# Two attentions and a mixture of experts on one core: a hand-placed order of steps replaced by a greedy one

## The chip, the core and the metric

One NeuronCore of a Trainium2 chip runs the whole program. It has five in-order instruction queues: TensorE (PE, with weight loads shown apart as PEld), VectorE (DVE), ScalarE (ACT), GpSimd (POOL) and SyncE (SP), which here only issues transfers. The metric is device time in microseconds (us), the median of several runs.

## The reference

The input x is 2 batches of 1024 tokens by 128 channels, in float32. The layer is, with all weights small:

```
x = layernorm(x + attention0(x))                  # 8 heads of 16, causal, plus a rank-one geometric bias
x = layernorm(x + ffn(x)), where ffn(x) is y with
    h = rmsnorm(x, norm1_w)
    q = rope(h Wq);  latent = layernorm(h Wdkv) * ln_g + ln_b   (64 wide)
    k = rope(latent Wuk);  v = latent Wuv
    x = x + softmax(causal(q k / sqrt(8))) v Wo   # 16 heads of 8
    g = rmsnorm(x, norm2_w)
    e = argmax(g gate_w + gate_b)                 # one of 4 experts per token
    y = x + W2[e] relu(W1[e] g + b1[e]) + b2[e]   # 512 hidden; all 4 experts are computed, one is picked
```

## The kernel before

Work is cut into **steps**, tuples such as `("scores", F, v)` or `("proj", M, 0)`. One global list, SCHEDULE, holds all of them. Each engine's program walks this list in order and emits the instructions of the steps in which it has a part, with semaphore waits for what it reads. The list thus sets the order on every queue; it does not set any time.

**Attention groups.** A group F is 4 heads of one batch: groups 0 and 1 are attention 0 of batch 0, groups 2 and 3 of batch 1, groups 4 to 7 attention 1 of batch 0, groups 8 to 11 of batch 1. For a group there are 38 `max` units (a matmul of queries against keys without the row maximum, L837, with a causal mask matmul L834, then a maximum on VectorE, L1238); then `combine`, `turnmax` (transpose L894 and a split into three bf16 parts) and `rows` (three DMAs put the negated maxima as rows into qs). Only then can the 38 `scores` units run (matmul L858, exponential on ScalarE L1024 into pr), `mask` on GpSimd (L752) for diagonal blocks, `pv` (12 products per group, L875), and per half of the queries `evac` (ScalarE, L1029) and `turn` (transposes L886, then reciprocal and product on VectorE, into att). Keys and queries of a group sit in one of three slots (qs, ks), filled by `load` DMAs from DRAM scratch.

**Chains.** Before attention 0, `before_first(b)` transposes x (`feed`, L912; `feat`), projects it (`proj`, L931), splits q and k into three bf16 parts (`hi`, `r1`, `mid`, `lo`) and stores them. Between the attentions, `between(b)` goes from the last `turn` of attention 0 of a batch to the stored q and k of attention 1. It handles both halves (512 tokens each) of the batch together: transposes of att, output product `y`, `residual`, `moments`, inverse root (`root`, four parts of linked small VectorE instructions, L1169 to L1176), `layer_norm` into x1 (L1281), `square` on ScalarE (L1070), `square_sum` on VectorE (L1288), a second root, `hat` on GpSimd (L792), transposes, `latent` and its normalisation (a third root), four rotated blocks M of q and k (`proj`, `rotate` L1313 on VectorE, `rotated` L773 on GpSimd through one buffer), their split and store, and the values. `ready` and `experts` do the same after attention 1, with `hidden` (L1004), `relu` (L1089) and `expert` (L948).

**The order around the change.** `backbone` writes the attention steps in a fixed pattern. A product follows the scores of its step by LAG = 2 steps. The maxima of group G are spread evenly over the run of group G-1, by MAX_SPREAD. The chains are spread evenly between two positions, where position F is the start of group F's scores: before_first(1) from -0.5 to 0.4, between(0) from 2.21 to 3.12, between(1) from 4.21 to 5.95, ready(0) and its experts from 8.21 to 11.7, ready(1) half 0 from 11.71, experts of batch 1 from 13. At 12.9 stands `quiet`, from where all eight PSUM banks serve the experts.

## Time and profile before

| | before |
|---|---|
| median of 3 runs | 675.29 us (673.31 to 678.19) |
| profiled execution | 673.76 us |
| its span in the trace | 671.9 us |
| mean granted TensorE clock | 0.954 |
| TensorE busy | 582.0 us (87%) |
| VectorE busy | 413.1 us (61%) |
| ScalarE busy | 337.8 us (50%) |
| GpSimd busy | 145.5 us (22%) |

The span runs from the first to the last instruction in the trace. Busy is time in which an engine has an instruction in work; a clock of 1 is 2.4 GHz, 0.5 is 1.2 GHz, and a value between is a mean over the stretch.

### The profile page before, as it was taken

The numbers are of one execution on the slowest core, as the hardware profiler recorded it, in microseconds if no ns is written. First come the engines' busy times: TensorE is split into PE (matmuls) and PEld (weight loads), VectorE is DVE, ScalarE is ACT, GpSimd is POOL, SyncE is SP. The second block draws the span as 40 slices with busy tenths as digits, with TensorE's granted clock in tenths as the row PEclk, the third lists the DMA queues.
The fourth block names the chain that finished last, engine by engine and source line by source line (L and its number), as shares of the span: only waits on it lengthen the run. The fifth ranks groups of instructions, "written<-read, shape, count | busy, mean of one in ns | idle before, by whom it ended". The sixth has DMA issues, their size and how long they took to land.

```text
span 671.9 us, 10096 instructions
## 1 busy us (share of the span) xinstructions
PE 582.0 (87%) x3668; PEld 279.0 (42%) x3717; DVE 413.1 (61%) x1031; ACT 337.8 (50%) x621; POOL 145.5 (22%) x186
## 2 busy tenths in 40 slices
PE   5578899958777877879999999999989999799994
PEld 3224233424223233424433344455544545357663
DVE  3496987796615968897778878754566402422313
ACT  4234457544463454557766667545546555633330
POOL 7612112313371031135321214011012011101000
PEclk9798899978787998999999999999999999989997
DMA  4856020000044020031313030220000000000000
GB/s 141 210 159 219 26 73 25 2 1 0 32 116 75 1 65 0 3 64 48 85 28 60 6 65 0 31 35 1 2 0 18 2 0 1 17 0 1 17 1 16
DMA packets 27394, 27.69 MB, mean 41 GB/s; under 512 B 6289, under 2 KB 22545, under 8 KB 27090
## 3 DMA queue, kind: packets, MB, share of 16 engines
q1 hardware_dynamic: 26962, 26.26, 16.2%
q0 software_dynamic: 384, 0.79, 0.5%
q8 instruction: 30, 0.49, 0.3%
q14 instruction: 18, 0.15, 0.1%
HBM read 19.40 MB, written 7.34 MB: 40 GB/s over the span
## 4 chain that ended last, share of the span: by engine, by line
PE 64%; DVE 20%; DMA 4%; issue 4%; ACT 4%; POOL 2%; SPq 1%; DVEq 0%; ACTq 0%; POOLq 0%
PE ps L875 13%; PE ps L948 10%; PE ps L858 10%; DVE mparts L1238 10%; PE ps L837 9%; PE ps L1004 8%; PE ps L834 3%; PE ps L937 3%; PE ps L931 2%; ACT pr L1024 2%; DMA qs<-nparts 2%; PE ps L912 2%; PE ps L946 2%; PE ps L886 1%; DVE stats L1147 1%
## 5 line engine op out<-in xcount | busy, mean ns | idle before, releaser
L1024 ACT ACTIVATE pr<-ps 128x512 f32<-128x512 f32 (+1 forms) x456 | 250.3, 576 | 227.9 <-PE ps L858 192.1
L1238 DVE TENSOR_REDUCE mparts<-ps 128x1 f32<-128x512 f32 (+3 forms) x456 | 279.9, 655 | 112.4 <-PE ps L837 111.2
L837 PE MATMUL ps<-ks,qs 125*128 125x512 bf16 (+3 forms) x576 | 170.0, 337 | 12.6 <-DVE mparts L1238 11.1
L858 PE MATMUL ps<-qs,ks 128*128 128x512 bf16 (+3 forms) x532 | 154.6, 332 | 15.7 <-ACT pr L1024 9.2
L752 POOL TENSOR_SCALAR_AFFINE_SELECT pr<-pr 128x512 f32<-128x512 f32 x96 | 61.0, 636 | 369.1 <-ACT pr L1024 368.9
L875 PE MATMUL ps<-pr,vs 128*32 128x512 f32 (+3 forms) x1152 | 126.4, 512 | 0.4 <-POOL pr L752 0.4
L858 PEld LDWEIGHTS ps<-qs,ks 128*128 128x128 bf16 x576 | 50.8, 99 | 143.2 <-ACT pr L1024 92.5
L834 PE MATMUL ps<-cmask,identb 128*128 128x128 bf16 (+2 forms) x259 | 64.9, 251 | 26.9 <-DVE mparts L1238 12.5
L837 PEld LDWEIGHTS ps<-ks,qs 125*128 125x128 bf16 x576 | 55.4, 100 | 53.1 <-DVE mparts L1238 21.2
L948 PE MATMUL ps<-w,work 128*128 128x128 f32 x512 | 74.1, 288 | 0.0
L1089 ACT ACTIVATE work<-ps,b 128x512 f32<-128x512 f32 x64 | 43.8, 686 | 49.1 <-PE ps L1004 48.5
L1004 PE MATMUL ps<-feat,w 128*128 128x512 f32 x128 | 63.9, 608 | 2.6 <-DVE att L1142 1.7
L948 PEld LDWEIGHTS ps<-w,work 128*128 128x128 f32 x512 | 61.9, 191 | 4.3
L834 PEld LDWEIGHTS ps<-cmask,identb 128*128 128x128 bf16 x264 | 26.3, 100 | 54.3 <-DVE mparts L1238 35.1
L1327 DVE SCALAR_TENSOR_TENSOR xn<-ps,onehot,xn 128x128 f32<-128x128 f32 x48 | 13.5, 344 | 48.0 <-PE ps L948 48.0
L875 PEld LDWEIGHTS ps<-pr,vs 128*32 128x32 f32 x1152 | 23.0, 109 | 46.9 <-issue 23.5
L1004 PEld LDWEIGHTS ps<-feat,w 128*128 128x128 f32 x128 | 23.6, 196 | 15.9 <-issue 12.6
L1138 DVE RECIPROCAL rc<-ps 128x16 f32<-128x16 f32 x24 | 6.1, 255 | 34.2 <-PE ps L886 33.8
L886 PE MATMUL ps<-ident,ot 128*128 128x128 f32 x96 | 16.9, 304 | 2.8 <-DVE mparts L1238 1.8
L946 PE MATMUL ps<-b2p,ones 3*128 3x128 bf16 x64 | 14.3, 224 | 3.7 <-ACT work L1089 3.6
L792 POOL TENSOR_TENSOR xn<-x,rstd 128x512 f32<-128x512 f32 x8 | 8.2, 1039 | 43.1 <-DVE rstd L1176 43.1
L785 POOL TENSOR_TENSOR parts<-work,parts 128x512 bf16<-128x512 f32 x12 | 13.9, 1156 | 13.9 <-ACT parts L1053 13.8
(119 smaller groups left out, 391.5 us busy)
## 6 DMA issues: line engine op xcount, KB each, us to landing
qs<-scr1q SPq DMA_DIRECT2D x64, 64.0 KB
ks<-scr1k SPq DMA_DIRECT2D x64, 64.0 KB
qs<-scr0q SPq DMA_DIRECT2D x48, 64.0 KB, 2.3
ks<-scr0k SPq DMA_DIRECT2D x36, 64.0 KB, 2.2
scr0q<-parts SPq DMA_DIRECT2D x4, 384.0 KB, 2.8
scr0k<-parts SPq DMA_DIRECT2D x4, 384.0 KB, 3.2
scr1q<-parts SPq DMA_DIRECT2D x4, 384.0 KB, 2.5
scr1k<-parts SPq DMA_DIRECT2D x4, 384.0 KB, 2.6
```

The costliest lines, as they stand in the source:

```text
L752: pool.affine_select(out=p, in_=p, compare_op=ALU.is_ge, fill=0.0, base=0, pattern=[[0, HG], [1, P]], channel_multiplier=-1).then_inc(done ...
L834: pe.matmul(bank[:, :, w - P:w], identb[:, :], cmask[:, 0:nh, :], start=True, stop=False, skip_group_check=True)
L837: last = pe.matmul(bank[:, h, :], queries(F, KMAX, h0 + h, i * P, P), ks[0:KMAX, F % SLOTS, h0 + h, 512 * c:512 * c + w], start=not diagon ...
L858: last = pe.matmul(to[:, h, :], ks[0:KEXP, F % SLOTS, h0 + h, j * P:(j + 1) * P], queries(F, KEXP, h0 + h, qb * 512 + lo, n), start=True, ...
L875: last = pe.matmul(ps[VW * h:VW * (h + 1), PVB, lo:lo + n], vs[:, F % VSLOTS, j, VW * h:VW * (h + 1)], pr[:, st % PSLOTS, h, 0:n], start=( ...
L886: last = pe.transpose(bank[:, t * P:(t + 1) * P], ot[:, q, t * P:(t + 1) * P], ident[:, :])
L946: pe.matmul(to, ones3[0:3, :], b2p[0:3, e * C:(e + 1) * C], start=True, stop=False, skip_group_check=True)
L948: last = pe.matmul(to, hid[:, e % 2, c, t * P:(t + 1) * P], w2[:, e * HC + c, :], start=False, stop=(c == HC - 1), skip_group_check=True)
L1004: pe.matmul(side(*step), w1[:, c * P:(c + 1) * P], feat[:, columns(b, i)], start=True, stop=True).then_inc(done["hidden"], 1)
L1024: act.activation(pr[:, st % PSLOTS, h0:h0 + nh, 0:STEPS[st][3]], scores_at(F, v), ACT.Exp, scale=GROUPS[F][0].scale).then_inc(exped, 1)
L1089: act.activation(hid[:, c // HC % 2, c % HC, :], side("hidden", b, i, c), ACT.Relu, bias=b1[:, c:c + 1]).then_inc(done["relu"], 1)
L1238: dve.tensor_reduce(mparts[:, F % SLOTS, h0:h0 + nh, i, c], maxes_at(F, u), AX_X, ALU.max).then_inc(taken, 1)
```

## The change

The positions stay as wishes only. `wanted` gives each step a position and each stream of dependent steps a lane, whose order is kept. `order` then builds SCHEDULE: it keeps a model of when each engine is free and when each step ends, from the table COSTS and the dependencies in `needs`, and repeatedly takes, among the heads of all lanes, the step with the smallest (wait in us on its first engine + 1.0 x its position). The maxima of a group may be wanted 1.2 groups ahead.

The chain between the attentions is cut in halves of 512 tokens, `between(b, i)`, each with its own roots. The first rms norm is folded into the layer norm: for x1 the root is taken of two values at once, 1/sqrt(v + eps) and 1/sqrt(v (1 + 1e-6) + 1e-11), and `hat0` on VectorE writes the doubly normalised values directly from xn; `square`, `square_sum`, the root and `hat` of the first rms norm go. x1 itself is written by four GpSimd instructions at the end of the chain. Blocks M of attention 1 are numbered half by half, and group 4 too is loaded in halves (HALVED). `ready(b, i)` works by halves as well. Products no longer have a fixed lag. The table's durations for scores, max and pv are linear in the columns; `halves_of_array` always gives both.

The diff, cut to its core (`needs`, which lists for each step kind the steps it reads from, the lanes and the changed semaphore waits are left out):

```diff
+def between(b, i):
+    q = block_of(1, b, 0, i)
+    k = block_of(1, b, 1, i)
+    return [("feed", "att0", b, i), ("feat", "att0", b, i), ("y", 0, b, i), ("residual", 0, b, i), ("moments", 0, b, i),
+            *root("x1", b, (i,)), ("hat0", b, i), ("feed", "hat0", b, i), ("feat", "hat0", b, i),
+            ("latent", b, i), ("lat_copy", b, i), ("proj", q, 0), ("rotate", q, 0), ("lat_moments", b, i),
+            *root("latent", b, (i,)), ("lat_norm", b, i), ("proj", q, 1), ("rotate", q, 1), ("rotated", q),
+            ("lat_turn", b, i), ("lat_feat", b, i), ("hi", q), ("r1", q), ("mid", q), ("lo", q), ("store", q),
+            ("proj", k, 0), ("rotate", k, 0), ("proj", k, 1), ("rotate", k, 1), ("rotated", k),
+            ("hi", k), ("r1", k), ("mid", k), ("lo", k), ("store", k), ("v_proj", 1, b, i), ("v_out", 1, b, i), ("x1", b, i)]
...
+MAX_AHEAD, MAX_LENGTH = 1.2, 0.9
-SECOND = (-0.5, 0.4)
-BETWEEN = [(2.21, 3.12), (4.21, 5.95)]
-AFTER = (8.21, 11.7)
-LAST = (11.71, 12.4)
+FIRST = [[(-2.0, -1.5), (-1.6, -1.1)], [(-0.5, 0.0), (-0.1, 0.4)]]
+BETWEEN = [[(1.2, 1.21), (2.0, 2.01)], [(3.4, 4.9), (4.1, 5.6)]]
+READY = [[(7.4, 7.9), (8.1, 8.4)], [(11.4, 11.6), (12.1, 12.2)]]
+EXPERTS = [[(7.9, 9.7), (9.7, 11.4)], [(11.6, 13.0), (13.0, 14.0)]]
...
+PE, DVE, ACTE, POOL, SP = "pe", "dve", "act", "pool", "sp"
+HOP = 0.07
+AFTER_ISSUE = {PE: 0.17, DVE: 0.0, ACTE: 0.0, POOL: 0.0, SP: 2.2}
+URGENT = 1.0
+def halves_of_array(step):
+    return 0, 1
+COSTS = {"feed": (PE, 0.58), "feat": (ACTE, 0.6), "proj": (PE, 0.87), "rotate": (DVE, 0.7), "rotated": (POOL, 1.27),
+         "hi": (ACTE, 0.62), "mid": (ACTE, 0.63), "store": (SP, 0.42), "v_proj": (PE, 1.14), "v_out": (ACTE, 0.6),
+         "combine": (DVE, 0.3), "rows": (SP, 1.0), "mask": (POOL, 0.64), "evac": (ACTE, 0.6), "y": (PE, 1.14),
...
+START = {PE: 5.0, DVE: 6.5, ACTE: 1.0, POOL: 6.4, SP: 4.5}
+X_READY = [5.0, 6.0, 7.0, 8.0]
...
+def order(wanted):
+    lanes = {}
+    for pos, stream, step in sorted(wanted, key=lambda e: e[0]):
+        lanes.setdefault(lane(stream, step), []).append((pos, step))
+    for name in lanes:
+        if name[0] == "projections":
+            lanes[name].sort(key=lambda e: e[1][1])
+    out, end, emitted_max = [], {}, {}
+    free = dict(START)
+    tile_free, issued, last_tile = [START[PE]] * 2, START[PE], None
+    ring, exps = [], []
+    bank_free, bank_reader, bank_use = {}, {}, {}
+    bank_held = {}
+    def ready(step, shared):
+        if kinds_left(step):
+            return None
+        times = []
+        for need in needs(step):
+            if need not in end:
+                return None
+            times.append(end[need] + HOP)
+        kind = step[0]
+        first = costs(step)[0][0]
+        if kind == "feed" and step[1] == "x":
+            times.append(X_READY[2 * step[2] + step[3]])
+        if kind in ("max", "turn", "turnmax"):
+            if len(ring) >= MAXN:
+                times.append(ring[-MAXN] + HOP)
+        if kind == "scores":
+            st, h0, _ = UNITS[step[2]]
+            if len(exps) >= SCN:
+                times.append(exps[-SCN] + HOP)
+            elif (SCB + step[2]) in bank_reader and bank_reader[SCB + step[2]] not in end:
+                return None
+            serial = step[1] * NS + st - PSLOTS
+            if serial >= 0 and ("pv", serial // NS, serial % NS) not in end:
+                return None
+        if kind == "pv" and step == ("pv", 0, 0) and PVB in bank_reader and bank_reader[PVB] not in end:
+            return None
+        if kind == "expert" and step[4]:
+            pass
+        elif kind in READER or kind == "proj":
+            bank = choose(shared)
+            if bank is None:
+                return None
+            if bank in bank_reader:
+                times.append(end[bank_reader[bank]] + HOP)
+        if first == PE:
+            own = halves_of_array(step) if kind in ("scores", "max") else (0, 1)
+            times += [tile_free[t] for t in own] + [issued]
+        else:
+            times.append(free[first])
+        at = max(times)
+        return at - max(issued, 0 if first == PE else free[first]), at
+    def kinds_left(step):
+        if step[0] == "combine":
+            F, q = step[1:]
+            return emitted_max.get(F, 0) < (NX0 if q == 0 else NX)
+        return False
+    def choose(shared):
+        able = [b for b in shared if b not in bank_reader or bank_reader[b] in end]
+        return min(able, key=lambda b: bank_use.get(b, -1)) if able else None
+    shared = [0, 1, *SIDE, PVB]
+    while any(lanes.values()):
+        best = []
+        for name, waiting in lanes.items():
+            if not waiting:
+                continue
+            picks = [0]
+            if name[0] == "max" and last_tile is not None:
+                F = name[1]
+                left = min(len(waiting), 6)
+                same_half = [k for k in range(left) if (waiting[k][1][2] < NX0) == (waiting[0][1][2] < NX0)]
+                picks = [k for k in same_half if last_tile not in halves_of_array(waiting[k][1])][:1] or [0]
+            for k in picks:
+                at = ready(waiting[k][1], shared)
+                if at is not None:
+                    best.append((at[0], waiting[k][0], name, k, at[1]))
+        _, pos, name, k, at = min(best, key=lambda x: max(x[0], 0.0) + URGENT * x[1])
+        step = lanes[name].pop(k)[1]
+        out.append(step)
+        kind, time = step[0], at
+        if kind == "scores" and step[1] == 0 and step[2] == 0:
+            shared = SIDE
+        if kind == "quiet":
+            shared = list(range(8))
+        if kind in READER or kind == "proj":
+            if not (kind == "expert" and step[4]):
+                bank = choose(shared)
+                bank_use[bank] = len(out)
+                if kind == "proj":
+                    bank_reader[bank] = ("r1", step[1]) if step[1] < 8 else ("rotate", step[1], step[2])
+                else:
+                    bank_reader[bank] = (READER[kind],) + step[1:4]
+        for k, (engine, cost) in enumerate(costs(step)):
+            if k:
+                time = max(time + HOP, free[engine])
+                if kind == "scores":
+                    serial = step[1] * NS + UNITS[step[2]][0] - PSLOTS
+                    if serial >= 0:
+                        time = max(time, end["pv", serial // NS, serial % NS] + HOP)
+            if engine == PE:
+                own = halves_of_array(step) if kind in ("scores", "max") else (0, 1)
+                issued = time + cost if len(own) == 2 else time
+                for t in own:
+                    tile_free[t] = time + cost
+                last_tile = own[0] if len(own) == 1 else None
+                if kind not in ("scores", "max"):
+                    last_tile = None
+            else:
+                free[engine] = time + cost
+            time += cost + AFTER_ISSUE[engine]
+        end[step] = time
+        if kind == "weights":
+            end[step] += 6.0
+        if kind in ("max", "turn", "turnmax"):
+            ring.append(time)
+        if kind == "max":
+            emitted_max[step[1]] = emitted_max.get(step[1], 0) + 1
+        if kind == "scores":
+            exps.append(time)
+    return out, end
+SCHEDULE, ENDS = order(wanted())
+MAX_ORDER = [[s[2] for s in SCHEDULE if s[:2] == ("max", F)] for F in range(NF)]
...
+                elif kind == "x1":
+                    b, i = args
+                    pool.wait_ge(done["root"], nth("root", "x1", b, (i,), 3))
+                    for t in range(TB * b + 4 * i, TB * b + 4 * i + 4):
+                        last = pool.tensor_scalar(x1[:, t, :], xn[:, t, :], mv[:, t, 0:1], rstd[:, 2, t:t + 1],
+                                                  ALU.subtract, ALU.mult)
+                    last.then_inc(done["x1"], 1)
...
-                    if of[:3] == "rms":
-                        dve.wait_ge(done["square_sum"], nth("square_sum", int(of[3]), b, blocks[-1]))
+                    if of == "rms1":
+                        dve.wait_ge(done["square_sum"], nth("square_sum", b, blocks[-1]))
+                        link(dve.tensor_scalar(rstd[:, 1, t], rstd[:, 5, t], 1.0 / C, RMS_EPS, ALU.mult, ALU.add))
                     elif of == "latent":
-                        dve.wait_ge(done["lat_moments"], nth("lat_moments", b, 1))
+                        dve.wait_ge(done["lat_moments"], nth("lat_moments", b, blocks[-1]))
+                        link(dve.tensor_scalar(rstd[:, 1, t], lat_mv[:, t, 1], 1.0, LN_EPS, ALU.mult, ALU.add))
                     else:
-                        which = 0 if of == "x1" else 2
-                        dve.wait_ge(done["moments"], nth("moments", which, b, blocks[-1]))
-                    link(dve.tensor_scalar(v, src, scale, eps, ALU.mult, ALU.add))
+                        dve.wait_ge(done["moments"], nth("moments", 0 if of == "x1" else 2, b, blocks[-1]))
+                        if of == "x1":
+                            link(dve.tensor_scalar(rstd[:, 1, t], mv[:, t, 1], 1.0 + RMS_EPS, LN_EPS * RMS_EPS, ALU.mult, ALU.add))
+                        link(dve.tensor_scalar(rstd[:, 0, t], mv[:, t, 1], 1.0, LN_EPS, ALU.mult, ALU.add))
...
+                elif kind == "hat0":
+                    b, i = args
+                    dve.wait_ge(done["root"], nth("root", "x1", b, (i,), 3))
+                    for t in range(TB * b + 4 * i, TB * b + 4 * i + 4):
+                        last = dve.tensor_scalar(x0[:, t, :], xn[:, t, :], mv[:, t, 0:1],
+                                                 rstd[:, 3, t:t + 1], ALU.subtract, ALU.mult)
+                    last.then_inc(done["hat0"], 1)
```

## Rows read from the trace of the kernel before

**Rows 1.** The page: span, and busy time, share and instructions of each engine.

```profile
span 671.9 us, 10096 instructions
...
PE 582.0 (87%) x3668; PEld 279.0 (42%) x3717; DVE 413.1 (61%) x1031; ACT 337.8 (50%) x621; POOL 145.5 (22%) x186
```

**Rows 2.** Windows: stretch, length, busy us of PE, PEld, DVE, ACT, POOL; clock, DMA share, GB/s.

```profile
0.00:38.50 38.50, 20.09 (x84) 10.82 (x86) 19.62 (x39) 11.91 (x21) 25.56 (x38) 0.91 0.64 171
38.50:98.10 59.60, 50.75 (x307) 19.45 (x310) 50.28 (x98) 27.83 (x53) 8.58 (x12) 0.94 0.37 117
98.10:129.50 31.40, 30.62 (x221) 11.65 (x224) 25.45 (x49) 21.11 (x41) 7.81 (x10) 1.00 0.10 27
129.50:196.00 66.50, 48.60 (x275) 22.79 (x280) 40.33 (x130) 31.89 (x61) 24.37 (x25) 0.83 0.11 28
196.00:209.00 13.00, 9.49 (x61) 4.02 (x62) 2.04 (x5) 5.81 (x12) 5.21 (x6) 0.76 0.52 98
209.00:246.50 37.50, 31.31 (x192) 11.18 (x193) 31.20 (x58) 16.10 (x30) 4.66 (x5) 0.97 0.20 38
246.50:334.60 88.10, 78.12 (x527) 34.74 (x535) 72.48 (x191) 52.75 (x101) 28.50 (x33) 0.98 0.17 40
334.60:397.20 62.60, 61.24 (x440) 23.20 (x447) 50.06 (x95) 42.02 (x81) 10.90 (x18) 1.00 0.21 37
397.20:549.30 152.10, 146.21 (x953) 75.32 (x968) 86.21 (x209) 84.01 (x156) 20.88 (x31) 1.00 0.08 13
549.30:585.90 36.60, 31.78 (x232) 16.15 (x233) 10.95 (x50) 20.97 (x39) 6.74 (x9) 1.00 0.03 8
585.90:672.00 86.10, 73.81 (x386) 49.67 (x385) 24.53 (x114) 23.34 (x35) 2.31 (x2) 0.92 0.02 7
```

**Rows 3.** The chain that ended last, 129.5 to 250: start us, us, what.

```profile
146.56 1.19 DVE rstd L1288 x2
...
151.64 1.05 POOL xn L792
...
188.65 1.27 POOL work L773
...
199.76 5.80 DMA ks<-scr1k
...
219.35 7.48 DVE mparts L1238 x13
```

**Rows 4.** The timeline of ScalarE, the two evacuation copies of group 1.

```profile
106.72 0.58 ACT L1029 COPY ot<-ps 128x512 f32<-128x512 f32 x1
...
128.84 0.58 ACT L1029 COPY ot<-ps 128x512 f32<-128x512 f32 x1
```

**Rows 5.** Groups by line: busy us, mean ns, idle before. Last two from 246.5:334.6 alone.

```profile
L1238 DVE TENSOR_REDUCE mparts<-ps 128x1 f32<-128x512 f32 (+3 forms) x456 | 279.9, 655 | 112.4 <-PE ps L837 111.2
...
L792 POOL TENSOR_TENSOR xn<-x,rstd 128x512 f32<-128x512 f32 x8 | 8.2, 1039 | 43.1 <-DVE rstd L1176 43.1
...
L1281 DVE TENSOR_SCALAR x<-xn,mv,rstd 128x128 f32<-128x128 f32 x16 | 4.9, 368 | 0.0
...
L1281 DVE TENSOR_SCALAR xn<-xn,mv,rstd 128x128 f32<-128x128 f32 x16 | 4.5, 342 | 0.1
...
L931 PE MATMUL ps<-work,wuk 128*128 128x512 f32 x8 | 4.2, 601 | 0.0
...
L992 PE MATMUL ps<-ident,work 128*64 128x128 f32 x8 | 1.2, 273 | 0.0
```

**Rows 6.** The timeline at the end: last matmuls, first instruction after moments, normalisation, store.

```profile
662.03 1.16 PE L948 MATMUL ps<-w,work 128*128 128x128 f32 x8
...
665.71 0.17 DVE L1169 TENSOR_SCALAR rstd<-mv 128x4 f32<-128x4 f32 x1
...
668.09 1.11 DVE L1281 TENSOR_SCALAR xn<-xn,mv,rstd 128x128 f32<-128x128 f32 x4
669.23 0.37 SPq L688 DMA_DIRECT2D out<-xn  x1
```

More of the change, by code:

```diff
@@ new lines, in attention @@
+    for F in range(NF):
+        passed, done = 0, {}
+        for v, (st, _, nh) in enumerate(UNITS):
+            out.append((F + passed / total, ("scores", F, v)))
+            passed += nh * STEPS[st][3]
+            done[st] = F + passed / total
+        for st in range(NS):
+            if STEPS[st][4]:
+                out.append((done[st], ("mask", F, st)))
+            out.append((done[st], ("pv", F, st)))
+            if st in END:
+                q = END.index(st)
+                out += [(done[st], ("evac", F, q)), (done[st], ("turn", F, q))]
@@ L338 @@
           "gate": "pick", "hidden": "relu", "expert": "pick_up"}
-LONG = {"layer_norm": 1.5, "hat": 2.0, "lat_norm": 2.0, "moments": 1.5, "pick": 1.5}
 def spread(steps, first, last):
-    total, passed, out = sum(LONG.get(s[0], 1.0) for s in steps), 0, []
-    for s in steps:
-        out.append((first + (last - first) * passed / total, s))
-        passed += LONG.get(s[0], 1.0)
-    return out
-def loads(position, F):
-    if F >= ATT[0].groups:
-        return [(position, ("load", F, k, 2)) for k in range(2)]
-    return [(position, ("load", F, k, i)) for i in range(2) for k in range(2)]
@@ L383, with halves_of_load, wanted, add @@
-SECOND = (-0.5, 0.4)
-BETWEEN = [(2.21, 3.12), (4.21, 5.95)]
-AFTER = (8.21, 11.7)
-LAST = (11.71, 12.4)
-SCHEDULE = schedule()
+    return [(first + (last - first) * k / len(steps), s) for k, s in enumerate(steps)]
+def halves_of_load(F):
+    return (0, 1) if F in HALVED else (2,)
+def wanted():
+    out = [(pos, "attention", s) for pos, s in attention() + maxima_steps()]
+    def add(stream, steps):
+        out.extend((pos, stream, s) for pos, s in steps)
+    for b in range(B):
+        for i in range(2):
+            add(("first", b, i), spread(before_first(b, i), *FIRST[b][i]))
+            add(("before", b, i), spread(between(b, i), *BETWEEN[b][i]))
+            add(("after", b, i), spread(ready(b, i), *READY[b][i]))
+            add("result", spread(experts(b, i), *EXPERTS[b][i]))
+    for F in range(NF):
+        for half in halves_of_load(F):
+            add("loads", [(max(-1.05, F - 1.9) + 0.01 * half, ("load", F, k, half)) for k in range(2)])
+    add("loads", [(F - 0.5, ("copy_v", F)) for F in range(NF)])
+    add("once", [(0.05, ("weights",)), (0.6, ("b2_parts",)), (0.7, ("partners",)),
+                 (-1.99, ("pads", 0)), (-1.98, ("pads", 1)), (-0.62, ("pads", 2)), (NF + 0.9, ("quiet",))])
+    add("once", [(F - 2, ("zeros", F)) for F in range(ATT[0].groups, ATT[0].groups + SLOTS)])
+    return out
@@ new lines, with lane @@
+OWN_LANE |= {kind: kind for kind in ("hidden", "relu", "expert", "pick_up", "x1", "x12", "scores", "pv", "mask", "copy_v", "quiet",
+                                     "pads", "zeros", "weights", "b2_parts", "partners")}
+def lane(stream, step):
+    kind = step[0]
+    if kind in ("max", "load"):
+        return step[:4] if kind == "load" else step[:2]
+    if kind in ("hi", "r1", "mid", "lo", "store"):
+        return "split", step[1]
+    if kind in ("proj", "rotate", "rotated", "v_proj", "v_out"):
+        return OWN_LANE[kind], step[1] >= (8 if OWN_LANE[kind] == "projections" else 1)
+    return OWN_LANE.get(kind, stream)
```

439 lines of the change are left out of this document (241 added, 198 removed).

## Prediction

> **What bounds the kernel now.** I read the clock and busy totals first, then a table of windows cut at the ends of attention groups, then the chain of work inside the worst window, then single durations. The totals [rows 1] name TensorE: 582.0 of 671.9 us busy, and no other engine over 61%. So an order of steps can win at most what TensorE idles (89.9 us), and what its clock loses when it idles. The profiled execution took 673.76 us, 1.86 us more than its span; the median of the runs is 675.29 us, 1.5 us above it. I make the sum against the span.
>
> The windows [rows 2] show where the idle time lies. A quiet stretch is 334.6 to 397.2: two groups (6 and 7) that do scores, products and maxima for a later group, with no other stream, in 62.6 us, TensorE busy 61.24. So a **plain group** is worth 31.3 us and has no slack left. Elsewhere:
> - 129.5 to 246.5 (three rows: 66.5, 13.0 and 37.5 us, together 117.0 us) is groups 2 and 3, with the chain between the attentions for batch 0 inside. TensorE is busy 48.60 + 9.49 + 31.31 = 89.4 us, so 27.6 us idle, and the granted clock falls to 0.83, 0.76 and 0.97: a mean of c between its two levels 1 and 0.5 costs (1 - c) of the window, here 11.3 + 3.1 + 1.1 = 15.5 us in which full-speed work was not done (part of it idle time as well).
> - 246.5 to 334.6 (88.1 us) is groups 4 and 5, with the same chain for batch 1: the same steps, 10.0 us idle, clock 0.98.
> - 0 to 98.1: 27.3 us idle, clock 0.91 and 0.94, with VectorE busy 50.28 of 59.6 us in its second part.
> - 397.2 to 585.9: 5.9 + 4.8 us idle. The tail from 585.9: 12.3 us idle, of which the last 9.9 us can't go: the last matmuls start at 662.03 and everything behind is one serial run of VectorE and a store [rows 6].
>
> In the worst window the chain of waits [rows 3] reads as one dependency after another: two square sums on VectorE, the GpSimd product by the root, half blocks rotated through one buffer, the copies of ks that land 5.80 us after 199.76, and only then 13 maxima back to back on VectorE. While those loads are awaited, 196 to 209, VectorE is busy 2.04 of 13.0 us. The maxima of group 4 cannot start before 205.6, and group 4 cannot score before they are done. The bound here is the latency of the chain for batch 0, from the last turn of group 1 at 129.5 to 205.6: 76 us.
>
> **The change, part by part.** 1. *The chain for batch 0 starts earlier and by halves.* The old order holds both halves until position 2.21. The first half needs only the first turn of group 1, whose evacuation copy is at 106.72; the second copy is at 128.84 [rows 4]. The new order asks for half 0 from 1.2 and half 1 from 2.0, so half 0 gets a lead of 22 us. Half 1 keeps its start but loses steps: the square sums from 146.56 to the end of the GpSimd product at 152.69 are 6.1 us, and a square before them; I take 8 us. One k block, not two, is rotated behind the second latent transpose (two such additions on GpSimd start some 5 us apart, one of them at 188.65 [rows 3]): 5 us. The steps that run for both halves in turn become single; some thirteen lie on the path (transposes, copies, projections, residual, moments, normalisations), each near the 0.6 us of a square sum (1.19 for two [rows 3]): 8 us, an estimate. 76 - 21 = 55 us, so the second halves of ks for group 4 land near 185. Behind that are the 27 maxima of the later query tiles at 0.655 us [rows 5] = 17.7 us, and about 7 us for combine, transpose, split and the row DMAs (219.35 + 7.48 to the start of group 4 at 246.5 has these and ten more maxima). Group 4 could start near 210, where it now starts at 246.5: 36 us.
>
> 2. *Is there engine time for it?* TensorE: two plain groups are 62.6 us and the chain's matmuls are 18.3 us (eight groups of rows in the window of batch 1; the largest and the smallest are in [rows 5]), 81 us against 117.0: 36 us again. VectorE: the window has 40.33 + 2.04 + 31.20 = 73.6 us busy, plus what is added, minus what moves into group 1 (25.45 of 31.4 busy, so 6 us of room): it would then be 90% busy. An end from below: groups 4 and 5 take 88.1 us with the same content. That is 29 us less than 117.0. I take 28 us, close to the stretch that really ran, because group 1 will be lengthened by what moves into it. Ends: 12 and 37.
>
> 3. *The chain for batch 1* moves from 4.21-5.95 to 3.4-4.9 and 4.1-5.6. Its window is 88.1 us against 81 us of matmuls: 4 us, ends -3 and 7.
>
> 4. *Start-up and groups 0 and 1.* The same chain of projection, split, store and load leads to the first scores; finer interleaving changes little, and VectorE is 84% busy from 38.5 to 98.1 with maxima that all must be done. 2 us, ends -4 and 6.
>
> 5. *Groups 8 to 11 and the tail.* The first experts of batch 1 may run from 11.6, in the last group (4.8 us idle of 36.6), where they now wait for 13. 4 us from the groups and 2 us from the tail, ends 0 and 9.
>
> 6. *Steps added and removed.* There are 16 inverse roots in place of 13: four each for x1, latent, second rms and result, where x1, first rms, latent and second rms had 2, 2, 2 and 3. One takes 668.09 - 665.71 = 2.38 us on VectorE [rows 6], so 7.1 us more, and one more small instruction in each of the four x1 roots (0.2 us each). Four square sums of 0.6 us go, and four squares on ScalarE. Net about +5.5 us on VectorE, in windows where it is 60 to 82% busy: 1 us on the path. The product of the first rms leaves GpSimd (1.04 us each [rows 5]), and the normalised x1 comes onto it, four instructions per half; their price isn't in the trace, between 0.2 us each (a fifth of the full product) and 1.04 us each. I take 0.4, 1.6 us a half, off the chain. A mask queued behind one waits that long, and a product with it: at most 4 x 4 us, taken as 0 because ScalarE runs ahead. The loads of group 4 become four in place of two, so 16 more DMA issues on SP in a queue idle there: 0.
>
> In the trace, the normalisation that runs with GpSimd active (x, at 368 ns) is 26 ns longer per instruction than the same one in the final result (342 ns) [rows 5]. The Trainium skill ("SBUF — State Buffer", Who interferes with whom) says that VectorE and GpSimd share one port pair under an exclusive lock, so that the second blocks fully. That speaks against moving x1 to GpSimd beside VectorE's hat0; By that rule the sixteen instructions of hat0 and those of x1 would run one after the other, up to 16 x 0.368 = 5.9 us. By the rows it is 16 x 0.026 = 0.4 us. The sum takes neither.
>
> 7. *The price of a greedy order.* Every queue is in order; where a real duration is longer than the table's, what is planned behind it waits. The table's maxima (0.1 + 512/880 = 0.68) and hidden steps agree with the trace; a matmul at the half clock takes twice what it says. I charge 3 us, ends 0 and 60 (below).
>
> Sum: 28 + 4 + 2 + 6 - 1 - 3 = 36 us. 671.9 - 36 = 635.9 of span, 637.8 us of time; I give **638**.
>
> **The rivals.** *VectorE or the chain takes the place of the wait.* The maxima of groups 2, 3 and 4 and two half chains meet on one in-order VectorE, and the latent roots of half 0 delay the maxima of group 2. For it: 13 maxima back to back on the chain [rows 3] and 81% in group 1. Against: batch 1's stretch keeps TensorE 89% busy at 82% of VectorE. It gives 12 us of the 28, and 4 us from the last groups: 671.9 - 12 - 4 + 3 + 1.9 = 661 us. *The whole forecast gain and the full bounds.* 37 + 7 + 4 + 8 and no misfit: 671.9 - 56 + 1.9 = 618 us.
>
> *Slower: the greedy rule undoes the lead of scores over products.* The old order keeps each product two steps behind its scores, whatever the durations, and plain groups are 98% busy [rows 2]. The greedy one places a product as soon as the table says the exponential and mask are done. There are 456 score units and 144 products; if each waits 0.1 us more because the real release is later than planned, that is 60 us, and the gain of 39 before misfit turns into 671.9 + 60 - 39 + 1.9 = 695 us. It decides from a mean wait of 0.065 us. Against it: a hand-over in the trace is short (the last normalisation ends at 669.20, its store is issued at 669.23 [rows 6], where the table allows 0.07), and maxima are nearly always at hand to fill a wait. *The order in effect stays as it was*, because the same dependencies release the same steps: 669 to 675.
>
> **Chances.** Forecast (626 to 650) 0.50; VectorE in its place (650 to 667) 0.22; the full gain 0.10; no effect 0.07; slower 0.11. The likeliest is 638. The range leaves out the slower case and no effect (0.18 together) and little more: 617 to 664. A difference of 1% is what can be told from none here; faster by more 0.82, within it 0.07, slower 0.11.
>
> **What would show it.** Group 4's first scores near 215 in place of 246.5; no window in 129.5 to 215 with VectorE under 30% busy; mean clock above the present 0.954; plain groups 6 and 7 still 31 to 32 us each; 16 roots; TensorE busy still near 580 minus what the clock gives back, at over 90% of the span. The prediction is wrong if the plain groups grow by more than 2 us each with TensorE waiting on exponentials, if the second half of ks lands after 200, or if the maxima of group 4 finish late because VectorE has no gap.

## The result, and the profile after

The changed kernel takes 656.07 us (median of 4 runs, 651.37 to 657.64) against 676.15 us for the kernel before (4 runs, 673.31 to 678.19). The ratio is 0.969, 95% interval 0.963 to 0.976. That is 20.1 us or 3.1% faster. The forecast was 638 us, 37 us under the 675.29 us it started from, so about half of it came.

The page of the changed kernel, which answers to [rows 1]:

```profile
span 649.6 us, 10160 instructions
...
PE 572.1 (88%) x3664; PEld 278.2 (43%) x3717; DVE 423.2 (65%) x1067; ACT 335.9 (52%) x617; POOL 153.8 (24%) x198
```

TensorE is 9.9 us less busy for nearly the same instructions, at a mean granted clock of 0.967 where the kernel before had 0.954; its idle time fell from 89.9 to 77.5 us. This page is of the fastest of the four executions. The other three had clocks of 0.950 to 0.953, and a second profiled execution of the same kernel (c0 below, clock 0.955) shows TensorE busy 577.2 us and idle 78.5. So the fall in idle time stands in both, and about half of the 9.9 us belongs to this one execution. VectorE is 10.0 us busier and GpSimd 8.3 us.

A second evacuation copy (ScalarE, line 1276 here, 1029 before) closes each group. The two of group 1, answering to [rows 4], and the second of group 0 stand in the timeline of ScalarE of the changed kernel:

```profile
105.35 0.58 ACT L1276 COPY ot<-ps 128x512 f32<-128x512 f32 x1
114.79 0.58 ACT L1276 COPY ot<-ps 128x512 f32<-128x512 f32 x1
152.01 0.58 ACT L1276 COPY ot<-ps 128x512 f32<-128x512 f32 x1 [0.37 <-PE ps L1119]
```

Subtracting the starts of successive second copies gives a length for every group. The rows of the changed kernel and of c0 are two executions of the same kernel. Groups 2, 3, 4, 6, 7 and the rest repeat to within 0.2 us, so there the table places an effect more sharply than the total does. Groups 0, 1 and 5 differ by 2.6, 2.1 and 1.2 us between the two, so a difference of that size there says nothing (us; groups 8 to 11 taken together; spans of one profiled execution each):

| kernel | group 0 | 1 | 2 | 3 | 4 | 5 | 6 | 7 | 8 to end of span |
|---|---|---|---|---|---|---|---|---|---|
| before | 97.5 | 31.3 | 66.6 | 50.4 | 48.7 | 39.4 | 31.3 | 31.3 | 275.4 |
| changed | 105.4 | 46.7 | 49.6 | 37.4 | 43.2 | 37.8 | 31.1 | 36.3 | 262.3 |
| c0, changed again | 107.9 | 48.8 | 49.5 | 37.4 | 43.4 | 39.0 | 31.1 | 36.3 | 262.3 |
| e1, rows first | 96.0 | 46.9 | 49.6 | 37.4 | 43.2 | 37.8 | 31.1 | 36.3 | 262.3 |
| e3, half 0 held | 106.2 | 31.9 | 56.8 | 39.7 | 43.4 | 39.7 | 31.1 | 36.3 | 262.3 |
| e6, both | 95.9 | 31.9 | 56.8 | 39.7 | 43.4 | 38.6 | 31.1 | 36.3 | 262.3 |
| e8, table corrected | 97.7 | 47.4 | 49.4 | 36.0 | 41.5 | 39.7 | 30.3 | 36.3 | 262.3 |
| e5, halves by hand | 97.5 | 31.3 | 72.2 | 51.1 | 63.0 | 37.8 | 31.3 | 31.3 | 279.3 |
| e7, weight 10 | 95.5 | 32.6 | 89.2 | 37.4 | 45.7 | 36.6 | 32.9 | 37.3 | 275.2 |

From before to changed: group 0 +7.8, groups 1 to 3 together -14.7, groups 4 and 5 -7.1, groups 6 and 7 +4.7, the rest -13.1, in sum -22.3 us, the difference of the two spans. Groups 2 and 3 alone lost 30.0 us, but 15.4 of these are back in group 1. The last two terms belong together too: experts now start in group 7, which lengthens it, and from the start of group 6 to the end 8.4 us are gained.

The windows of the changed kernel, cut close to its own group ends, answer to [rows 2] (columns as there):

```profile
0.00:43.70 43.70, 25.95 (x111) 13.99 (x113) 22.46 (x44) 14.07 (x24) 27.30 (x40) 0.88 0.74 160
43.70:106.00 62.30, 43.20 (x273) 15.49 (x276) 45.37 (x90) 23.41 (x44) 6.15 (x9) 0.86 0.30 97
106.00:152.70 46.70, 40.27 (x258) 17.05 (x262) 37.28 (x100) 25.41 (x48) 17.80 (x20) 0.96 0.15 43
152.70:202.30 49.60, 43.31 (x266) 19.53 (x269) 39.58 (x104) 25.79 (x48) 19.99 (x21) 0.93 0.14 43
202.30:239.60 37.30, 35.35 (x249) 15.53 (x251) 32.23 (x81) 23.60 (x46) 9.60 (x11) 1.00 0.19 33
239.60:320.70 81.10, 74.02 (x504) 32.10 (x512) 71.26 (x174) 50.03 (x96) 31.52 (x39) 1.00 0.17 47
...
537.20:580.50 43.30, 39.25 (x250) 18.86 (x253) 13.60 (x59) 26.16 (x48) 7.38 (x10) 1.00 0.02 7
580.50:649.60 69.10, 59.35 (x329) 40.84 (x328) 21.90 (x101) 18.86 (x28) 2.30 (x2) 0.96 0.03 8
```

The three windows from 106.0 to 239.6 idle TensorE for 14.7 us at a clock of 0.93 and more; the matching stretch before idled it 28.4 us at down to 0.76. TensorE's work there is nearly the same, 118.9 us against 120.0. Of the 14.7 us, 5.3 end with work of ScalarE (4.5 of it exponentials), 4.5 with VectorE and 3.1 with a mask on GpSimd, each in waits of 2.1 us or less: no engine stands out. VectorE is busy 82% of these windows, 67% before. The second row is the surprise: 19.1 us idle and clock 0.86 in group 0, where the kernel before had 8.9 us at 0.94. The chain of waits, read inside that window, shows one hole:

```profile
56.88 9.14 DMA scr0q<-parts
66.03 0.34 SPq L858
...
68.76 2.62 DMA scr0k<-parts
71.40 0.30 SPq L858
...
74.09 0.55 SPq L908
...
75.32 1.76 DMA qs<-nparts
77.08 0.45 issue
77.53 0.63 PE ps L1102
```

A store of projected q is issued on SyncE at 56.88 and takes 9.14 us to land. Behind it on the same in-order queue stands a load of group 2 that reads it, then the next store, then a load that reads that one, and only at 74.09 the row DMAs (L908) with the negated maxima of group 0. These had been ready since 59.5 (the last split instruction on VectorE starts at 59.24 and takes 0.28), and group 0's second half of scores waits for them.

The slow landing isn't new. In the kernel before, the same kind of store, issued behind the same bulk loads, took 9.1 us too (last number of its line in the list of transfers issued from 43 to 60 us):

```profile
scr0q<-parts SPq DMA_DIRECT2D x1, 384.0 KB, 9.1
```

The timeline of SyncE there:

```profile
47.59 0.49 SPq L660 DMA_DIRECT2D scr0q<-parts  x1
54.65 1.82 SPq L671 DMA_DIRECT2D qs<-nparts  x3
...
57.13 3.48 SPq L621 DMA_DIRECT2D qs<-scr0q  x6
```

The rows (L671) left while that store was still on its way, and the loads that read it stood behind them. What is new is the order on the queue. The window of the hole in the changed kernel:

```profile
60.40:77.50 17.10, 1.21 (x4) 0.33 (x4) 5.60 (x13) 0.00 (x0) 0.00 (x0) 0.59 0.52 171
```

TensorE does 1.21 us of work in 17.1, ScalarE and GpSimd none, and the mean granted clock is 0.59.

### The profile page after: what moved, and what is told of

Same layout as the page of the kernel before. It is cut to its first block, busy times and chain, and to the rows that moved or that the text cites. A ratio compares the mean times of both kernels' runs of the same rounds, so it can differ in the third digit from the quotient of the medians.

```text
span 649.6 us, 10160 instructions
## 1 busy us (share of the span) xinstructions
PE 572.1 (88%) x3664; PEld 278.2 (43%) x3717; DVE 423.2 (65%) x1067; ACT 335.9 (52%) x617; POOL 153.8 (24%) x198
## 4 chain that ended last, share of the span: by engine, by line
PE 66%; DVE 12%; ACT 7%; DMA 4%; issue 4%; POOL 4%; SPq 2%; DVEq 0%; ACTq 0%; POOLq 0%
PE ps L1119 14%; PE ps L1102 11%; PE ps L1195 11%; PE ps L1081 10%; PE ps L1251 8%; DVE mparts L1485 7%; ACT pr L1271 6%; PE ps L1078 3%; PE ps L1184 3%; PE ps L1178 2%; PE ps L1193 2%; PE ps L1130 2%; DMA scr0q<-parts 1%; POOL pr L989 1%; DMA scr0k<-parts 1%
## 5 line engine op out<-in xcount | busy, mean ns | idle before, releaser
L1485 DVE TENSOR_REDUCE mparts<-ps 128x1 f32<-128x512 f32 (+3 forms) x456 | 276.5, 654 | 96.2 <-PE ps L1081 95.0
L1081 PE MATMUL ps<-ks,qs 125*128 125x512 bf16 (+3 forms) x576 | 162.5, 335 | 15.9 <-DMA ks<-scr0k 10.4
L1102 PE MATMUL ps<-qs,ks 128*128 128x512 bf16 (+3 forms) x528 | 144.7, 325 | 25.1 <-DMA qs<-nparts 13.6
L1119 PE MATMUL ps<-pr,vs 128*32 128x512 f32 (+3 forms) x1152 | 122.7, 500 | 8.7 <-POOL pr L989 4.0
L1102 PEld LDWEIGHTS ps<-qs,ks 128*128 128x128 bf16 x576 | 49.4, 97 | 109.9 <-ACT pr L1271 72.7
L1333 ACT ACTIVATE work<-ps,b 128x512 f32<-128x512 f32 x64 | 43.9, 687 | 36.8 <-PE ps L1251 36.3
L1119 PEld LDWEIGHTS ps<-pr,vs 128*32 128x32 f32 x1152 | 23.6, 108 | 49.5 <-issue 24.6
L1251 PEld LDWEIGHTS ps<-feat,w 128*128 128x128 f32 x128 | 22.9, 190 | 13.6 <-issue 8.4
L1130 PE MATMUL ps<-ident,ot 128*128 128x128 f32 x96 | 15.1, 281 | 2.7 <-DVE mparts L1485 2.6
L1276 ACT COPY ot<-ps 128x512 f32<-128x512 f32 x24 | 14.0, 583 | 6.6 <-PE ps L1119 6.5
L971 POOL MEMSET qs<- 32x4096 bf16 x3 | 10.5, 3504 | 24.2 <-PE ps L1102 24.1
```

The source lines that it names most:

```text
L1081: last = pe.matmul(bank[:, h, :], queries(F, KMAX, h0 + h, i * P, P), ks[0:KMAX, F % SLOTS, h0 + h, 512 * c:512 * c + w], start=not diagon ...
L1102: last = pe.matmul(to[:, h, :], ks[0:KEXP, F % SLOTS, h0 + h, j * P:(j + 1) * P], queries(F, KEXP, h0 + h, qb * 512 + lo, n), start=True, ...
L1119: last = pe.matmul(ps[VW * h:VW * (h + 1), PVB, lo:lo + n], vs[:, F % VSLOTS, j, VW * h:VW * (h + 1)], pr[:, st % PSLOTS, h, 0:n], start=( ...
L1130: last = pe.transpose(bank[:, t * P:(t + 1) * P], ot[:, q, t * P:(t + 1) * P], ident[:, :])
L1251: pe.matmul(side(*step), w1[:, c * P:(c + 1) * P], feat[:, columns(b, i)], start=True, stop=True).then_inc(done["hidden"], 1)
L1333: act.activation(hid[:, c // HC % 2, c % HC, :], side("hidden", b, i, c), ACT.Relu, bias=b1[:, c:c + 1]).then_inc(done["relu"], 1)
```

## The experiments

All ratios are to the kernel before, run on the same chip. The kernel as changed was run again as a yardstick.

> The changed kernel unedited, as the yardstick for the three edits that run beside it. Both theories expect 656 us, a ratio to the kernel before of 0.970, and TensorE without work from about 60 to 77 us.

Measured: 655.58 us, ratio 0.969 (0.963 to 0.974).

**Rows first.** Only SyncE's order is edited, the plan of all computing engines stays:

```diff
 SCHEDULE, ENDS = order(wanted())
+ROWS_AT = SCHEDULE.index(("rows", 0, 1))
+LATE = [s for s in SCHEDULE[:ROWS_AT] if s in (("load", 2, 0, 1), ("store", 7), ("load", 2, 1, 1))]
+SCHEDULE = [s for s in SCHEDULE[:ROWS_AT + 1] if s not in LATE] + LATE + SCHEDULE[ROWS_AT + 1:]
```

> One edit: on SyncE's queue the three row DMAs of group 0's second half go ahead of the last two loads and the last store of the batch-1 keys and queries, which stand before them in the changed kernel. Theory A (the 17 us hole from 60.3 to 77.5 is head-of-line blocking on SyncE): the rows land near 62.5 instead of 77.1, the hole shrinks to under 3 us, the maxima of group 2 start some 5 us later than their loads now allow, and the kernel takes 641 to 647 us (10 to 15 us less). Theory B (VectorE's maxima bound groups 0 to 2, the hole only shows it): the idle time reappears behind the maxima and the kernel takes 653 to 657 us.

Measured: 642.56 us, ratio 0.949 (0.945 to 0.954), 13.0 us less than the yardstick. SyncE's timeline of this kernel:

```profile
55.97 0.49 SPq L900 DMA_DIRECT2D scr0q<-parts  x1
58.87 1.84 SPq L911 DMA_DIRECT2D qs<-nparts  x3
66.94 2.69 SPq L861 DMA_DIRECT2D qs<-scr0q  x6
```

The rows go out at 58.87, and the load that still waits for its store until 66.94 no longer holds them. Theory A holds for the time (641 to 647 us) and for the order as the cause. Group 0 shrinks to 96.0 us and the other groups keep the lengths of the changed kernel. But the rows don't land near 62.5 as expected: they land between 65.4 and 67.4, 6.5 us after their issue in the median:

```profile
scr0q<-parts SPq DMA_DIRECT2D x1, 384.0 KB, 11.0
qs<-nparts SPq DMA_DIRECT2D x3, 4.0 KB, 6.5
```

In the changed kernel, issued at 74.09, the same three took 1.8 us. So TensorE's longest wait for the row DMAs falls from 13.3 to 4.3 us and not to nothing. This edit together with the later weights of e2 was not run.

**Expert weights later.**

```diff
 def weights():
...
-                for dst, src in [(w1[:, :], "W1T"), (w2[:, :, :], "W2T"), (b1[:, :], "b1T")]:
-                    sp.dma_start(dst, a[src]).then_inc(moe_in, 16)
 def move_b2():
...
+                for dst, src in [(w1[:, :], "W1T"), (w2[:, :, :], "W2T"), (b1[:, :], "b1T")]:
+                    sp.dma_start(dst, a[src]).then_inc(moe_in, 16)
```

> One edit: the transfers of W1, W2 and b1 (2 MB) are issued behind the move of b2 instead of with the other weights. Theory A1 (the store of block 6 takes 9.14 us to land because it shares the DMA engines with these weights, and the planner counts 2.2 us): the store lands in 2.5 to 4 us, the hole shrinks by 5 to 8 us, the kernel takes 648 to 652 us. Theory A2 (only the order on SyncE's queue matters, the rows wait for the stores anyway): the store still takes over 7 us or the hole keeps over 14 us, and the time stays at 654 to 658 us.

Measured: 651.98 us, ratio 0.966 (0.960 to 0.971), 3.6 us less than the yardstick, with intervals that overlap. The chain of waits of this kernel shows where the rest went:

```profile
56.95 5.79 DMA scr0q<-parts
...
65.48 4.40 DMA scr0k<-parts
...
72.59 0.55 SPq L908
```

The first store takes 3.35 us less to land, the second 1.78 us more than in the changed kernel, and the rows leave at 72.59 in place of 74.09. So the 2 MB of W1 and W2 account for part of the 9.14 us. What makes the rest was not tried (cos and sin, 512 KB each, are issued in the 2.4 us before the store). Without W1 and W2 the queue's order still makes a hole: TensorE waits 10.6 us for the rows. Neither theory's numbers are met in full: the landing lies between them, the time too.

**The table told the truth.**

```diff
         if kind == "weights":
             end[step] += 6.0
+        if kind == "store" and step[1] in (6, 7):
+            end[step] += 7.0
```

> One edit in the planner's model: the stores of blocks 6 and 7 land 7 us later than it thinks, as the trace shows for block 6 (9.14 us). The planner then puts the rows ahead of the second-half loads of group 2 by itself. Theory A (a wrong entry in the table made the hole): 641 to 648 us, hole under 3 us. Theory B (the greedy rule makes another such hole somewhere else as the order shifts): 650 us or more.

Measured: 642.69 us, ratio 0.951 (0.948 to 0.953). The planner now places the rows ahead of the late loads by itself, and gets the same time as the hand edit. So the wrong place of the rows came from the entry of 2.6 us from issue to landing. The hole itself is not under 3 us, as expected, but 8.7: the rows leave at 59.26 behind both stores, which take 11.4 and 11.9 us to land here, and themselves need 7.8 us. The time equals e1's because the new plan balances it: groups 0, 1 and 5 are longer by 4.1 us in all, groups 3, 4 and 6 shorter by 3.9.

**Half 0 held.**

```diff
-        return {"att0": [("turn", last_group(0, b), i)],
+        return {"att0": [("turn", last_group(0, b), i if b else 1)],
```

> One edit in the planner's dependencies: half 0 of the batch-0 chain between the attentions may not start before the last turn of group 1, as in the kernel before; the order is planned anew. Theory A (the early start of half 0 carries the gain of groups 1 to 3): groups 2 and 3 lengthen again and the kernel takes 664 to 672 us. Theory B (the gain comes from the single first-rms-free chain by halves and from the planner's filling, not from the early start): 655 to 660 us, group 1 shortens by what groups 2 and 3 lengthen.

Measured: 647.72 us, ratio 0.958 (0.953 to 0.962), 7.9 us *faster* than the yardstick. Neither theory had a time that low. The windows at its group ends:

```profile
106.16:138.03 31.87, 30.56 (x223) 12.09 (x225) 26.12 (x51) 21.15 (x42) 8.19 (x10) 1.00 0.15 44
138.03:194.81 56.78, 47.65 (x296) 23.51 (x299) 47.98 (x151) 30.20 (x58) 28.83 (x31) 0.94 0.14 46
194.81:234.51 39.70, 36.88 (x256) 16.24 (x258) 32.98 (x83) 23.79 (x46) 9.75 (x11) 1.00 0.20 35
```

Group 1 is a plain group again (31.9 us, clock 1.00), and groups 1 to 3 take 128.4 us in place of 133.7. The early start of half 0 cost 5.3 us in this plan. It did not earn anything here.

**Both.** This has the two edits together.

> Both edits that helped: the rows ahead of the late loads on SyncE, and half 0 of the batch-0 chain held until the last turn of group 1. If they are independent (13.0 and 7.9 us): 634 to 637 us, groups 1 to 3 at 128 us and group 0 near 96. If holding half 0 helped only because the hole delayed group 1's work: 640 to 643 us.

Measured: 637.32 us (636.99 to 638.88), ratio 0.943 (0.939 to 0.946). The two savings (13.0 and 7.9 us) add up within 3 us, and this is the fastest kernel of the study, 18 us under the changed one.

**The halves without the planner.** The new steps at fixed positions, with the old backbone and, but for what the diff shows, the old positions:

```diff
-SCHEDULE, ENDS = order(wanted())
...
+    for b in range(B):
+        for i in range(2):
+            out += spread(between(b, i), *HALVES[b][i])
...
+HALVES = [[(2.21, 2.75), (2.5, 3.12)], [(4.21, 5.1), (4.75, 5.95)]]
+SCHEDULE = schedule()
```

> The chain by halves alone: the new steps (single halves, first rms folded in, group 4 loaded in halves) put at fixed positions with the old backbone, batch 0 from 2.21 to 3.12 and batch 1 from 4.21 to 5.95, in place of the planner. Theory A (the shorter chain by halves carries groups 1 to 3): groups 1 to 3 take 128 to 136 us in place of 148, group 0 stays at 97.5, and the kernel takes 655 to 663 us. Theory B (the planner's filling carries it): groups 1 to 3 take over 142 us and the kernel takes over 668 us.

Measured: 697.83 us, ratio 1.032 (1.028 to 1.036). Theory A falls: groups 1 to 3 take 154.6 us. Three of its windows:

```profile
129.40:201.70 72.30, 51.68 (x281) 24.22 (x282) 40.65 (x142) 30.76 (x59) 26.21 (x27) 0.86 0.10 31
201.70:252.80 51.10, 41.26 (x255) 13.65 (x256) 33.13 (x62) 21.78 (x41) 12.32 (x15) 0.93 0.24 49
252.80:315.70 62.90, 49.30 (x293) 24.39 (x293) 44.72 (x129) 27.34 (x53) 17.27 (x20) 0.84 0.15 32
```

At these positions the shorter chain leaves 20.6 us idle in group 2 (17.9 before) and 13.6 in group 4. TensorE stands at steps of the chain: 9.3 us in two waits for the normalised values. These positions weren't tuned and the steps of a block aren't interleaved as the old list had them, so this says that the halves alone, at the old positions, earned nothing; what the best hand order would give stays open.

**Position over wait.** Both edits, and `URGENT = 10.0` in place of 1.0.

> Rows first, half 0 of batch 0 held, and the planner's weight on the wished position is 10 us per group in place of 1, so that a step is taken for its position rather than for a short wait. Theory A (the gain is the greedy filling of waits): the idle time of TensorE in groups 2 to 5 grows and the kernel takes 642 to 660 us. Theory B (any order from the dependency model does, the weight is of no matter): 635 to 640 us.

Measured: 682.89 us, ratio 1.010 (1.006 to 1.014). First scores come at 58.4 us, and group 2 is longer than in any other kernel:

```profile
128.80:218.00 89.20, 60.69 (x308) 28.31 (x313) 55.17 (x157) 32.11 (x59) 29.95 (x31) 0.81 0.10 32
```

28.5 us idle, clock 0.81. Both expected ranges (642 to 660 and 635 to 640 us) were too low. With the same steps, table and dependencies, the weight alone is worth 46 us: 32 of them in group 2 and 13 from group 8 on. What gains is taking the step that can go now.

**Start-up order.** Both edits; the loads of group 1's first half and the third `pads` go behind all loads of group 0.

```diff
+BEHIND = [s for s in SCHEDULE if s in (("load", 1, 0, 0), ("load", 1, 1, 0), ("pads", 2))]
+SCHEDULE = [s for s in SCHEDULE if s not in BEHIND]
+AT = max(SCHEDULE.index(("load", 0, 0, 1)), SCHEDULE.index(("load", 0, 1, 1))) + 1
+SCHEDULE = SCHEDULE[:AT] + BEHIND + SCHEDULE[AT:]
```

> On top of the two edits of the best kernel so far (rows first, half 0 held: 637 us): the loads of group 1's first half and the third padding memset go behind all loads of group 0, as in the kernel before. Theory A (the first scores come at 43 to 45 us in place of 38.5 because other transfers stand ahead of group 0's on SyncE and GpSimd): first scores at 38.5 to 40, 633 to 636 us. Theory B (VectorE's maxima set the pace of group 0, so the later start costs nothing): group 0 still ends near 96, 637 us.

Measured: 639.38 us, ratio 0.946 (0.940 to 0.951), level with e6. First scores come 1.4 us sooner (41.2), group 0 ends 1.9 us sooner, and group 5 is 2.6 us longer in this execution. The range of Theory A (633 to 636 us) is missed: this edit gave group 0 at most 2 us and the kernel nothing.

**Batch 1 held too.**

```diff
-        return {"att0": [("turn", last_group(0, b), i)],
+        return {"att0": [("turn", last_group(0, b), 1)],
```

> Rows first and half 0 held until the last turn for both batches, not batch 0 alone. Theory A (starting half 0 early buys nothing in either chain, the planner fills as well without it): 636 to 640 us, groups 3 to 5 together at 119 to 123 us as in the kernel with batch 0 held. Theory B (in batch 1, where VectorE has room, the early half pays): groups 3 to 5 lengthen by 4 us or more, 641 us or more.

Measured: 643.72 us, ratio 0.952 (0.949 to 0.955), 6.4 us slower than e6. Groups 3 to 5 take 127.9 us (35.4, 44.8, 47.7) in place of 121.7. 9.1 of this is in group 5 and 4.3 were won back in group 3. So in batch 1 the early half pays, as Theory B expected. That it does because attention 1 of batch 0 is at hand as filler is argued, not shown.

**No expert of batch 1 before the last turn.**

```diff
     if kind == "hidden":
-        return [("feat", "hat1", *a[:2]), ("lo", 15), ("v_proj", 1, 1, 1), ("weights",)]
+        return [("turn", NF - 1, 1)] * a[0] + [("feat", "hat1", *a[:2]), ("lo", 15), ("v_proj", 1, 1, 1), ("weights",)]
```

> One edit in the planner's dependencies: no hidden matmul of a batch-1 expert before the last turn of group 11, as in the kernel before. Theory A (the last groups and the tail gained because experts of batch 1 fill TensorE in group 11): the last group and the tail together lengthen by 4 to 8 us, 660 to 664 us. Theory B (only some six of them ran ahead, the gain is from the halves of the second chain and a shorter tail): under 2 us, 655 to 658 us.

Measured: 658.39 us, ratio 0.975 (0.970 to 0.979). The total is within its noise of the yardstick. The last evacuation copy shows it better, in e4:

```profile
573.80 0.59 ACT L1276 COPY ot<-ps 128x512 f32<-128x512 f32 x1 [1.19 <-PE ps L1119]
```

Group 11 takes 34.0 us in place of 43.3, and the stretch behind its copy 83.1 (656.9 - 573.8) in place of 69.8: 4.0 us more together, the low end of Theory A. That is what experts running ahead into the last group earn.

**x1 on VectorE.** On e6, with the table changed to VectorE, 1.4 us.

> On top of the best kernel (rows first, half 0 held: 637 us): x1 is written by four VectorE instructions per half in place of GpSimd's (804 ns each in the changed kernel, 3.2 us a half), and the table says so. Theory A (x1 on GpSimd delays masks, and products behind them, more than 1.1 us per half costs VectorE): 633 to 636 us. Theory B (VectorE is the scarcer engine between the attentions, GpSimd's price is hidden): 637 to 641 us, groups 2 to 5 up to 4 us longer.

Measured: 647.02 us, ratio 0.959 (0.952 to 0.965), 9.7 us slower than e6, from groups 2 (59.2), 3 (41.0) and 5 (45.6). Theory B has the sign, and its range (637 to 641 us) is missed. Of the profiled difference 7.0 us are in group 5, which moves by as much in plans without this edit, so the run does not price the choice of engine.

A caution on e3 to e11: each constraint gives another plan, and group 5 alone went from 38 to 48 us in them. A few microseconds between two plans are not the price of one edit. e1 and e2 keep the plan.

## Why the prediction was half right

The measured 656 us lies in the range (617 to 664), with the forecast sign, but outside the forecast's own band (626 to 650) and inside that of the VectorE rival (650 to 667). The time forecast was too low by 18 us. Of the named signs, plain group 6 at 31.1 us and the 16 roots came, and VectorE is busy 66% or more in every 13 us from 129.5 to 207.5 and 84% from there to 215. The clock was above 0.954 only in the fastest execution, TensorE was busy 88% of the span and not over 90, and group 4's scores start near 239, not 215. By its steps:

**Steps 1 and 2 (28 us from groups 2 and 3)** took the right window and read it alone. Groups 2 and 3 gave 30.0 us, yet group 1 grew by 15.4 of chain steps moved into it; over the three the gain is 14.7 us (12.6 in c0). The prediction said that group 1 would lengthen, and subtracted about 1 us for it (29 to 28). The term is mis-sized by half. It asked for all the idle time of groups 2 and 3 (27.6 us) to go, while of 28.4 in the three groups 14.7 stay. The chain itself got shorter by more than the forecast 21 us. From the last copy of group 1 to the issue of the last ks load for group 4 it was 70.9 us (128.84 to 199.76), and is 43.6 (152.01 to 195.59, the last of these eight loads):

```profile
193.21 2.68 SPq L858 DMA_DIRECT2D ks<-scr1k  x8
```

In e1 that load leaves at 186.4, where the forecast had the landing near 185. But here group 1 ends 23.2 us later than before, 7.8 from group 0 and 15.4 of its own, and in group 3 TensorE is busy 35.35 of 37.3 us: there its own work bounds the group, not the chain. One reason given for the term was wrong as well: "half 0 gets a lead of 22 us" was the first argument, and e3 shows that without the lead the three groups take 5.3 us less, 19.9 us under before. Group 4 needs the second half too, which starts at the last turn in either case; that this is why the lead earns nothing is argued, not shown.

**Step 4 (start-up and group 0, 2 us, ends -4 and 6)** is the step that failed outright: group 0 cost 7.8 us, outside its bounds (10.4 in c0). The diff moved batch-1 loads ahead of the rows on SyncE's queue, and the prediction looked on that queue only at the 16 extra issues of group 4. The landing time of a store under load, 9.1 us in the trace of before, was not looked up either. Undone in e1, group 0 takes 96.0 us, 1.5 less than before: the 2 us of the step, and the gap to the forecast is closed to 5 us. With e3's edit as well, the kernel takes 637.3 us. That this is the forecast 638 is luck: it needs an edit that takes back the early half on which the forecast built.

**Step 3 (batch 1, 4 us, ends -3 and 7)** gave 7.1 us, just above its upper end, and 5.7 in c0, inside it.

**Step 5 (late groups and tail, 6 us)** gave 8.4 us with groups 6 and 7 counted in; half of it is experts in group 11 (e4: 4.0 us).

**Step 6.** VectorE is 10.0 us busier, not 5.5. The roots and squares are as counted; slower instructions, below, more than make up the rest (the latent normalisations 2.8 us, one held instruction 2.7). The price of x1 on GpSimd was taken at 0.4 us per instruction, between 0.2 and 1.04; it is 0.80:

```profile
L1028 POOL TENSOR_SCALAR x<-xn,mv,rstd 128x128 f32<-128x128 f32 x16 | 12.7, 804 | 4.7 <-DVE rstd L1423 4.7
```

3.2 us a half. Products waited 4.0 us in all for a mask on GpSimd (0.4 us before), so the 0 charged for masks behind x1 was a little low. The wait falls from 1.9 us in e6 to 0.8 in e11, where x1 is off GpSimd; e11 was slower all the same, and doesn't settle which engine is the right one.

**Step 7 and the slower rival.** The plain group 6 runs in 31.1 us, 31.3 before. The greedy order keeps scores and products apart as well as the fixed lag did. What breaks it is the mechanism that step 7 itself names, a real duration longer than the table's with work planned behind it. It was charged 3 us, and one entry cost 13 (e1), in one place and not a tenth of a microsecond in 600. So the loss shows in step 4's window and belongs to step 7's term.

**The VectorE rival** (661 us) had the nearest time, partly by luck. It gave 12 us of the 28 and the three groups gave 14.7. But its mechanism doesn't bound either place: in the hole VectorE was idle for 11.5 of 17.1 us, and in groups 1 to 3 only 4.5 of the 14.7 us that TensorE idles end with VectorE.

**The rival of the full gain** (618 us) was added from 4 us for the start-up and 8 for the late groups, where steps 4 and 5 state ends of 6 and 9; with these it would be 615 us. Nothing hangs on it.

## What to carry to other kernels

An order planned from a table of durations can be undone by one wrong entry, and here it was a transfer's landing time while others ran (2.6 us in the table, 9.14 in the trace). Give stores the landing that the trace shows under load, and look at each in-order DMA queue for an urgent small transfer behind one that waits. When work moves from one window to an earlier one, sum over both. A shorter chain pays only if something else can fill the time around it: at fixed positions the halves earned nothing (e5), and the early start of the first half cost 5.3 us in batch 0 (e3) and paid in batch 1 (e10).

## What the hardware showed unexpectedly

Some VectorE instructions that read and write SBUF were held while GpSimd worked. The same latent normalisation takes 529 ns a piece in the changed kernel, 357 ns before. Eleven of its sixteen instructions take 301 to 311 ns. The other five take 664 to 1326, and each of these ends 0.05 us behind the end of an elementwise sum or difference or a mask on GpSimd. Beside x1's instructions on GpSimd two of them took 303 and 311 ns. TensorE waited 2.1 us for one of these normalisations, and 4.3 us for two in e1. The plainest case, from the timeline of the changed kernel:

```profile
236.44 3.50 POOL L971 MEMSET qs<- 32x4096 bf16 x1 [14.88 <-PE ps L1102]
...
237.09 2.88 DVE L1410 TENSOR_SCALAR rstd<-lat_mv 128x4 f32<-128x4 f32 x1
...
240.01 0.17 DVE L1417 TENSOR_SCALAR rstd<-rstd 128x4 int32<-128x4 int32 x1
```

An instruction on four columns, 0.16 us elsewhere, takes 2.88 us and ends at 239.97, when the memset ends (239.94). By the rule that the prediction quoted (the Trainium skill, "SBUF — State Buffer", Who interferes with whom), one engine holds the shared port pair for a whole instruction, and here the trace agrees. For the pair that the prediction weighed it doesn't:

```profile
164.14 1.17 DVE L1536 TENSOR_SCALAR x<-xn,mv,rstd 128x128 f32<-128x128 f32 x4
164.21 3.23 POOL L1028 TENSOR_SCALAR x<-xn,mv,rstd 128x128 f32<-128x128 f32 x4 [2.35 <-DVE rstd L1423]
```

Four instructions of hat0 beside four of x1 take 1.17 us (1.11 with GpSimd idle, at 225.95) and 3.23 us (3.13 without hat0, at 245.09). Nothing was blocked. Why the one pair collides and the other doesn't was not tried.
